# A two-layer gated attention kernel: outer weight of the last layer rounded in halves, result copies ahead of a rounding, and LoRA steps moved

## The reference

```python
x = x + tanh(g_xattn[1]) * L1_xattn(layernorm(x), ctx)          # last attention
x = x + tanh(g_ffn[1]) * L1_ffn(layernorm(x))                   # last feed-forward

logits = x @ gate_W.T + gate_b;  top1 = argmax(softmax(logits))
base = x @ wi_W.T + wi_b                                        # 256 -> 1024
for i in range(8):
    inter = relu(base + (x @ lora_A[i].T) @ lora_B[i].T)
    out += (top1 == i) * (inter @ wo_W.T + wo_b)                # 1024 -> 256
```

## Time and profile before

| What | Value |
|---|---|
| Median of 3 runs | 854.37 us (853.56 to 856.18) |
| Profiled execution, its own time | 851.03 us |
| Span of its instructions | 848.9 us |
| Busy share of PE, DVE, ACT, POOL | 91%, 68%, 55%, 26% |
| Mean granted clock of PE | 0.971 of full speed |
| Chain that ended last, by engine | PE 68%, DVE 12%, DMA 5%, ACT 4% |
| Last attention step | 727 to 755 us of the span |
| Last feed-forward | 751 to 849 us of the span |

### The profile page before, as it was taken

The page is one execution under the profiler, slowest core; times in us unless marked ns, Lnnn a source line. Parts: engine busy times, 40 slices in busy tenths (PEclk is TensorE's granted clock), DMA queues, the critical chain, the costliest instruction groups (busy, mean ns, idle before and its releaser), DMA issues.

```text
span 848.9 us, 22217 instructions
## 1 busy us (share of the span) xinstructions
PE 770.1 (91%) x7992; PEld 602.9 (71%) x7992; DVE 580.6 (68%) x1773; ACT 470.7 (55%) x1014; POOL 218.2 (26%) x212
## 2 busy tenths in 40 slices
PE   5879999999999888779998679998999998889997
PEld 2547777777777665469996457777777776569996
DVE  4877778777787677744545778887888777574433
ACT  2455665656556467335663346665666666555553
POOL 2562322133232305700005444224312112010000
PEclk9999999999999999989999869999999999899999
DMA  8898878678776904623325778887978888000001
GB/s 197 178 231 208 179 162 162 147 164 177 163 172 139 217 8 126 186 84 101 119 91 131 154 159 167 203 173 150 201 171 182 188 188 184 12 1 1 20 20 39
DMA packets 153765, 117.87 MB, mean 139 GB/s; under 512 B 81574, under 2 KB 145170, under 8 KB 153650
## 3 DMA queue, kind: packets, MB, share of 16 engines
q1 hardware_dynamic: 146410, 107.93, 56.1%
q0 software_dynamic: 4096, 6.57, 3.1%
q10 hardware_dynamic: 3152, 1.96, 1.0%
HBM read 76.17 MB, written 38.30 MB: 135 GB/s over the span
## 4 chain that ended last, share of the span: by engine, by line
PE 68%; DVE 12%; DMA 5%; issue 4%; ACT 4%; SPq 4%; ACTq 1%; POOL 1%; DVEq 0%; POOLq 0%
PE ps L1981 21%; PE ps L2125 9%; PE ps L2099 8%; PE ps L2158 6%; PE ps L2148 6%; PE ps L2182 3%; PE ps L2144 3%; DVE mx L1589 2%; DVE ps L1585 2%; DMA scr_q<-qp 2%; ACT prob L1020 2%; PE ps L2052 2%; DMA QS<-scr_q 1%; PE ps L2168 1%; PE ps L2040 1%
## 5 line engine op out<-in xcount | busy, mean ns | idle before, releaser
L1020 ACT ACTIVATE prob<-ps 128x400 f32<-128x400 f32 (+1 forms) x384 | 182.3, 499 | 87.6 <-PE ps L2148 81.1
L2125 PE MATMUL ps<-KS,QS 96*100 96x361 bf16 x512 | 164.9, 338 | 16.1 <-DMA QS<-qp 4.7
L1585 DVE CUSTOM_DVE_ANT_0 ps<-ps,biasq 100x361 f32<-100x361 f32 x256 | 135.3, 542 | 50.7 <-PE ps L2125 46.8
L1589 DVE TENSOR_REDUCE mx<-ps 100x1 f32<-100x361 f32 x256 | 126.9, 527 | 42.2 <-PE ps L2125 41.2
L2148 PEld LDWEIGHTS ps<-QS,KS 98*128 98x128 bf16 x1536 | 108.7, 100 | 50.1 <-ACT prob L1020 8.9
L2148 PE MATMUL ps<-QS,KS 98*128 98x100 bf16 x1536 | 133.2, 210 | 7.5 <-ACT prob L1020 4.6
L2099 PE MATMUL ps<-cT,wk 128*128 128x361 f32 x256 | 96.2, 486 | 7.5 <-PEq L2394 6.8
L2125 PEld LDWEIGHTS ps<-KS,QS 96*100 96x100 bf16 x512 | 63.8, 126 | 51.3 <-DVE mx L1589 15.4
L730 POOL TENSOR_TENSOR kp<-kr,kp 128x722 bf16<-128x722 f32 x32 | 48.7, 1521 | 184.8 <-ACT kp L991 184.6
L2158 PE MATMUL ps<-prob,V 128*17 128x100 f32 (+1 forms) x3072 | 82.0, 256 | 0.1
L2158 PEld LDWEIGHTS ps<-prob,V 128*17 128x17 f32 (+1 forms) x3072 | 66.5, 99 | 12.6 <-issue 9.4
(11 more groups left out here) (225 smaller groups left out, 1610.8 us busy)
## 6 DMA issues: line engine op xcount, KB each, us to landing
scr_k<-kp SPq DMA_DIRECT2D x93, 180.5 KB, 4.2
KS<-scr_k SPq DMA_DIRECT2D x62, 270.8 KB, 4.0
cT<-in_ctxT SPq DMA_DIRECT2D x32, 361.0 KB, 4.3
KS<-scr_k SPq DMA_DIRECT2D x62, 180.5 KB, 4.2
QS<-scr_q SPq DMA_DIRECT2D x60, 150.0 KB, 3.9
KS<-scr_k SPq DMA_DIRECT2D x62, 90.2 KB, 4.4
scr_q<-qp SPq DMA_DIRECT2D x42, 100.0 KB, 4.6
xg<-scr_x SPq DMA_DIRECT2D x32, 128.0 KB
```

The lines of the kernel that those rows point to most:

```text
L1020: nc.scalar.activation(prob[0:KROWS[t], t, hg, :], ps[0:KROWS[t], c % 2, 0:HQ * S], ACT.Exp).then_inc(a["exp"], 1)
L1585: nc.vector.tensor_tensor_reduce(ps[0:S, banks[h % len(banks)], 0:S2], ps[0:S, banks[h % len(banks)], 0:S2], biasq[p][:, :], 1.0, -3.0e38, ...
L1589: nc.vector.reduce_max(mx[:, h:h + 1], ps[0:S, banks[h % len(banks)], 0:S2], axis=AX.X).then_inc(a["max"], 1)
L2125: mm(ps[0:S, banks[h % len(banks)], 0:S2], QS[p][0:SROWS, h, :], KS[p][0:SROWS, h * S2:(h + 1) * S2], start=True, stop=True).then_inc(a["s ...
```

## The change

The outer weight is split in two halves of four inner tiles. ACT rounds the first in the last attention step, behind `norm(F1N, 0)` and ahead of the exponentials of the third head group, and the second where it rounded the whole. DVE makes the low part of the first half behind those of the inner and the LoRA weight, and that of the second behind the first `hidden_low`. PE waits for each half ahead of the first `down1` that reads it. In every group but the first, ACT copies the results of the group before ahead of the rounding of the second tile, no longer behind it, and PE waits for each of the two copied banks where it first writes it. Of the LoRA steps, `lora_low(2)` moves from behind tile 7 to behind tile 5 of group 1, and some parts of `choose`, `turn_lora(3)`, `copy_lora(3)` and `lora_low(3)` move later.

```diff
@@ ACT, step
                         high(s1, *EARLY[1][:2])
                         norm(F1N, 0)
+                        high(s1, woh[:, 0:NFT1 // 2, :], woT[:, 0:NFT1 // 2, :])
                 exps(l, b, 2, range(NKT))
@@ ACT, behind attn(1)
-            high(s1, woh[:, :, :], woT[:, :, :])
+            high(s1, woh[:, NFT1 // 2:, :], woT[:, NFT1 // 2:, :])
@@ ACT, hidden
                 nc.scalar.activation(hh[i % 2][:, :], ps[:, i % 2, 0:GT], ACT.Relu, bias=wib[:, i:i + 1]).then_inc(s1["h"], 1)
+                if g > 0 and i == 1:
+                    copy_y(g - 1, 0, GT)
                 act.wait_ge(s1["h"], START + n + 1)
                 act.wait_ge(s1["y"], START + n + 1)
@@ ACT, loop
                     hidden(i, g)
-                    if g > 0 and i == 1:
-                        copy_y(g - 1, 0, GT)
...
-                    if g == 2 and i == 1:
+                    if g == 2 and i == 3:
                         copy_lora(GE)
@@ DVE, attn
                         low(s1, j + 1, wl, w[r], wh[r])
+                    low_out(0)
                     stats_end(F1N, GE * GB, B - 1)
@@ DVE
+            def low_out(half):
+                t = slice(half * NFT1 // 2, (half + 1) * NFT1 // 2)
+                low(s1, 3 + half, wol[:, t, :], woT[:, t, :], woh[:, t, :])
...
-            low(s1, 3, wol[:, :, :], woT[:, :, :], woh[:, :, :])
...
                     hidden_low(i, g)
+                    if g == 0 and i == 0:
+                        low_out(1)
...
                     if g == 0:
-                        if i == 0:
-                            choose(1, (0,))
                         if i == 1:
                             norm(F1N, GE)
                         if i == 2:
-                            choose(1, (1,))
+                            choose(1, (0, 1))
...
                         if i == 5:
+                            lora_low(2)
+                        if i == 6:
                             choose(GE, (1,))
-                        if i == 6:
+                        if i == 7:
                             choose(GE, (2,))
-                        if i == 7:
-                            lora_low(2)
-                    if g == 2 and i == 2:
+                    if g == 2 and i == 5:
                         lora_low(GE)
@@ PE
             def down1(i, g):
-                if i == 0:
-                    pe.wait_ge(s1["y_copied"], START + KT * g)
                 pe.wait_ge(s1["lo"], START + NFT1 * g + i + 1)
+                if g == 0 and i in (0, NFT1 // 2):
+                    pe.wait_ge(s1["wlo"], START + 3 + 2 * i // NFT1)
                 for m in range(KT):
+                    if i == 0 and g > 0:
+                        pe.wait_ge(s1["y_copied"], START + KT * (g - 1) + m + 1)
...
-                        if i == 2:
-                            pe.wait_ge(s1["wlo"], START + 3)
...
-                    if g == 2 and i == 0:
+                    if g == 2 and i == 1:
                         turn_lora(GE)
```

## The result

| | before | after |
|---|---|---|
| Median of 5 runs | 855.22 us | 848.82 us |
| Ratio to before, 95% interval | | 0.9922, 0.9896 to 0.9948 |
| Profiled execution | 851.03 | 849.73 |
| Span, mean granted clock | 848.9, 0.971 | 847.9, 0.974 |

The interval says 4.4 to 8.9 us; 4.9 were predicted. A second comparison of the same kernels gave 0.9932 (0.9899 to 0.9966).

The account below looks back on a forecast made before the run. In the last feed-forward PE's instruction list was taken as the bound, broken by few waits. Gains of 2.2 + 1.1 + 0.65 + 0.65 + 0.28 = 4.9 us gave 849.5 us, range 847.6 to 852.6.

Parts of the forecast that it names:

- Part 1: Last attention step: ACT's rounding of the first half delays exponentials and PE's score matmuls, a loss of 0.7 us (0.5 to 1.05).
- DVE's cover: Attention's end: the half's low part costs nothing; low tokens at 751.4, PE wants them at 751.9, 0.4 us to spare.
- Part 2: Feed-forward start: idle 1.72 before down1(0, 0) goes; down1(1, 0) gains 2.2 us net (bounds 1.4 to 2.85).
- what is late next is `xn`: Last group's transposes: POOL's steps end at 759.5, xn at 760.95, so down1(1, 0) starts at 761.15.
- a gain of 1.9: Feed-forward start: POOL held behind hlo, the half and the next hlo, rstd at about 759.8.
- rival (a): Slow clock stretch moves to the attention or transposes instead of going, costing 1.4 to 1.6 us: 851.0; chance 0.22.
- Part 3: LoRA steps: earlier lora_low(2) removes the idle before lora1(0, 2), gaining 1.1 us (0.8 to 1.2).
- Part 4: Group boundaries: copies ahead of the rounding let down1 start earlier, gaining 0.28, 0.65 and 0.65 us.
- Rival (d): Boundary gaps have another cause; Part 3 and Part 4 give 1, Part 2 gives 1.5: 851.9; chance 0.07.
- rival (b): POOL's first step at the feed-forward start takes 2.1 us by itself; gain 4.1, 850.3; chance 0.10.
- (e): Longer pause at 740 drops the clock until the feed-forward; at 12 us costs 11, about 855 to 860; chance 0.03.
- Rival (c): Pause at 740 is absorbed and xn isn't late; 0.5 to 0.9 us more gain, 848.8; chance 0.06.

Follow-up runs that it names:

- rounded twice: Changed kernel, with ACT also rounding the second half in the attention step and again later; tail 107.54 us, against 105.15 for the changed kernel.
- LoRA steps alone: Kernel before, with only the LoRA rounding of group 2 earlier and group 3's LoRA steps later; ratio 0.9975, tail 109.57 us against 110.45.
- copies alone: Kernel before, with only the result copies ahead of the second tile's rounding and a wait for each bank; ratio 0.9975, tail 108.01 us against 110.45.
- halves only: Changed kernel with copies and LoRA steps put back, leaving the outer weight in halves; ratio 0.9963, tail 107.73 us against 110.45 before.
- low part first: Changed kernel, with DVE making the second half's low part ahead of the first hidden_low; tail 105.83 us against 105.15.
- one wait: Changed kernel, with PE waiting once for both copied banks; tail 105.38 us against 105.15.
- half in the gap: Changed kernel, with ACT rounding the first half ahead of the outputs' copy and DVE's low part behind lora_low(0); ratios 0.9924 and 0.9944, tails 105.00 us.
- LoRA matmul ahead: Kernel of half in the gap, with PE's first-tile LoRA matmul ahead of the last output projection; ratio 0.9932, tail 104.74 us.
- low part later: Kernel of LoRA matmul ahead, with DVE's low part of the second half behind norm(F1N, 3); ratio 0.9940, tail 106.46 us.

## Why the prediction was right

**Time.** 849.5 predicted, 848.82 measured; the tail is 5.3 shorter, 4.9 predicted. That the two times lie within 0.7 is partly luck: the prediction started from a median of 854.37, the comparison has 855.22, and the medians differ by 6.4.

**Part 1** was right in mechanism and size: 0.69 for 0.7, on the path one to one (rounded twice: 0.94 for 0.96). The place behind the token copy was the flaw of the change, not the half: in a gap 8 us on (ACT's idle 1.53 ahead of 753.14) it is free. DVE's cover held as well: its low tokens were done at 755.43, PE began on the tokens at 756.17.

**Part 2** was 0.5 too small. `down1(1, 0)` came 2.72 earlier, 2.2 was predicted, 2.85 the bound without a late `xn`. The term that was mis-sized is "what is late next is `xn`": it held `down1(1, 0)` back by 0.65 in the sum (761.15 for 760.5) and by nothing in the profile, where the transposes follow PE's LoRA matmul at once. It rests on a smaller one: I let the relu start 0.18 earlier for the shorter rounding ahead of it, from the length of the first of two LoRA matmuls. It starts 0.57 behind that matmul's start in both kernels (754.33 and 754.90, 759.31 and 759.88), so the rounding had not held it. DVE therefore stood idle for 0.18 ahead of its first `hlo`, and POOL was in ahead of it. The hold itself, for which I took a middle value, is shown by three kernels: 1.05 for the first step beside half the work, 2.34 for both steps when `hlo` comes right behind, 1.69 with the low part out of the way. The Trainium skill (GPSIMD Engine Reference, Specifications) says only that the two engines contend, which the trace bears out; that POOL would be held behind one such piece of DVE work after another, for a gain of 1.9, was my reading of it, and it did not come true. The second step ran beside the end of `hlo` and then for 0.9 us beside `wol`, and took 1.20 for 1.04.

What I had left in the background is the clock. I wrote that the slow stretch goes "with it, I take it", left it inside the 2.2, and gave its price, 1.4 to 1.6, only in rival (a). Of the 2.72, 1.45 are clock and 1.3 the wait less what the half cost, and the 1.45 are there only in executions in which the clock falls: it did in the kernel before and in the LoRA steps alone, not in the copies alone. **Rival (a)** came true in none of five profiles with the pause of 1.16 (the changed kernel twice, halves only, low part first, one wait), but did at a pause of 2.1 us at the same place.

**Part 3**: 1.1 predicted, 1.05 alone. **Part 4**: 1.58 for three boundaries predicted, 1.65 alone. Rival (d) falls with these two, rival (b) with POOL's 0.23, and (e) with a clock at 1.00 from 745 on. Where the clock did fall at that place, in the kernel that rounds twice, it cost 1.56 and not (e)'s 11. Rival (c) came true by half: `xn` wasn't late, the pause was not absorbed.

**What stays open**: the times of the half in the gap, the LoRA matmul ahead and the low part later don't order these kernels. The profiles say that the half in the gap saves 0.69 over the change, at an equal clock. A fall of the clock is worth more than that, and how often it comes in each kernel would take many profiles of each. Why it fell behind the idle 1.72 in two profiles and not in the third is not shown.

## What to carry to other kernels

Ask of each engine's idle stretch on which side of a released instruction it lies: ACT had 1.53 us to spare 8 us on, and the half cost its full time because it stood right ahead of the exponential that PE waited for. When a wait is removed, its price has two parts, the idle time and the slow clock behind it; give them apart, since the second is not there in every execution. And look at what POOL does while DVE is handed two-input work: an earlier relu cost 0.6 us at the next place, because it closed the gap on DVE through which POOL had slipped.

## What the runs showed of the hardware

POOL's first step, on 100x4 elements, takes 0.23 us when no DVE work on two SBUF tensors is running as it starts. When such work is running, it ended 0.1 us behind that work's end: it took 2.115 beside a piece of 2.27 us, 1.05 beside one of 1.21, 0.40 beside an `hlo` of 0.56. The second step, which lasts 1.04 elsewhere, ended 0.89 or 0.90 behind the end of the DVE instruction that was running as it started, in all five orders that were profiled (before, after, low part first, LoRA matmul ahead, low part later). The DVE instruction after that one did not hold it. So it took 1.20 when it started under the last 0.3 us of `hlo`, with most of `wol` still to come, and 1.86 when it started under `wol` itself. DVE's `hlo` took 0.55 to 0.60 with POOL beside it or not. What holds a POOL step is thus the one DVE instruction that runs as it starts, and not how much of such work follows.

The row of DVE before the change that belongs to the second step of the earlier trace rows, which ends at 759.56:

```profile
758.10 0.57 DVE L1834 TENSOR_TENSOR hlo<-hh,hhi 128x400 fp32r<-128x400 f32 x1
```

One execution of the unchanged kernel took 1843 us. Its page gives a matmul of line 2125 a mean of 643 ns where others have 338, while DVE's reductions hold their time. The profile gives a granted clock of 1.00 throughout, but it holds no record of the clock at all for this execution (20 in the first profile of this kernel), so the 1.00 may only mean that nothing was recorded. The slowing also goes beyond the 1.2 GHz level: 128x400 matmuls follow at 0.44 us and more near its end, where the slow stretches have 0.33. A granted clock of 1.00 is therefore no proof of full speed; look at the spacing of the matmuls as well. The cause was not looked for.

```profile
PE 1814.5 (99%) x7992; PEld 1216.7 (66%) x7992; DVE 591.4 (32%) x1773; ACT 491.6 (27%) x1014; POOL 215.5 (12%) x212
...
L2125 PE MATMUL ps<-KS,QS 96*100 96x361 bf16 x512 | 315.1, 643 | 2.9 <-DVE mx L1589 2.0
```
